# A GRU scan behind a mixture of experts: output turns placed behind the product of their window, one gate seed moved, and sixteen VectorE instructions in every step

## The chip, the cores and the metric

The kernel runs on one core of one Trainium2 chip. The metric is the device time of one execution in microseconds (us); the number that counts is the median over executions.

## The reference

The input `x` is [2, 1024, 256] in float32, with a condition vector of 256 per batch entry. Two layers follow, each added to its input:

```
# layer 0: four experts (two picked per batch entry) and a shared one
for e in range(E):                      # E = 4, hidden width 1024
    h = gelu(context_c @ ew1[e] + eb1[e])
    out = out + w_be[:, e] * mask[e] * (h @ ew2[e] + eb2[e])
out = out + gelu(context_c @ sw1 + sb1) @ sw2 + sb2
# layer 1: a GRU over the 1024 tokens, state h of 256 per batch entry
def step(h, xs):
    z = sigmoid(xzt + h @ U_z + vz)
    r = sigmoid(xrt + h @ U_r + vr)
    hh = tanh(xht + r * h @ U + vh)
    return (1.0 - z) * h + z * hh
```

The GRU is a chain of 1024 steps, and each needs the state that the step before it made.

## The kernel before

The 1024 tokens are cut into 16 chunks (`CH`) of 64 (`CT`). After a start of some 54 us, which computes layer 0 for chunk 0, the kernel runs one loop of 1024 steps. Step s is token t of chunk c. In each step TensorE multiplies the state by the three recurrent matrices (split into two float16 parts), and in two windows beside that it does the work of layer 0 for the next chunk: window 0 lies between the products of Z and those of C, window 1 lies behind the products of C. The list `SIDE[t, w]` says what stands in a window: one unit in window 0, two in window 1. Units are UP and DOWN (half a tile of the two expert matrices), BIAS, PROJECT (the input part of the gates) and IDLE.

The chain of one step runs over three engines. TensorE makes the sum of gate R; ScalarE takes its tanh (`gate_tanh`); VectorE makes `p_cur`, the reset state; TensorE multiplies it for gate C; ScalarE takes that tanh; VectorE's scan writes the new state `h_cur`. Gate Z goes beside it: `z_sum`, a tanh on ScalarE, and two instructions that write `blend`, from which the scan reads.

VectorE's own order in a step is: `p_cur` (L618), `z_sum` (L626), `p_low` (L629), a fill that clears a place in the bank of Z (L632), `blend` twice (L636 and L638), the scan (L644), `h_two` twice (L647 and L648, the second is the cast to float16), `half_h` (L649), and `out_feat` (L654). An instruction can carry one wait for a semaphore itself. Where the code asks for more, the others stand in wait instructions of VectorE's sequencer ahead of it, up to two semaphores in one. There are three of these in a step, at L617, L635 and L643, so a step has 14 instructions. The semaphore `blended` counts three times in a step: at each `blend` and at `half_h`. The semaphore `part_ready` counts six times: at `p_cur`, `p_low`, the fill, the scan, and the two `h_two`, the cast last (`H_HIGH16`).

Some steps have an instruction more on VectorE. `seed` copies a gate's bias over a bank of the next chunk, at the places named in `SEEDS`: (t, 1) is behind the blends of step t, (t, 0) is at the end of step t-1, behind `out_feat`. `residual` adds the sum of layer 0 to the features, twice per chunk. GpSimd multiplies the tiles of `hidden` by the expert weights (`scale_tile`, L283), after ScalarE's gelu.

Every 16 steps a TURN transposes the finished outputs on TensorE (`turn_body`, L758). It stands first in window 1 of t = 1, 17, 33 and 49, ahead of the window's one other unit, and it waits for `blended`, that is, for the second `blend` of its own step.

Of the kernel before, what the change touches and what calls it, by code (L numbers as in the profile page):

```python
# [15 lines left out]
P = 128  # L16
GATES = 3
R, Z, C = range(GATES)
# [14 lines left out]
H_FILL = 20  # L33
IDLE_FILL = (256, 384)
IDLE_AT = 128


def moe_gru_kernel(nc, x, cond, gate_w, gate_b, time_w, time_b, ew1, eb1, ew2, eb2, sw1, sb1, sw2, sb2,
                   w_z, u_z, c_z, b_z, w_r, u_r, c_r, b_r, w_h, u_h, c_h, b_h, branch_mask, out):
    B, T, D = x.shape  # L40
    E, _, H = ew1.shape
    BR = E + 1
    KC = D // P
    CT = TOKENS
    CH = T // CT
# [24 lines left out]


    FIRST_BRANCHES = [e for e in (0, 1, 3, 4, 2) if any(on for *_, on in token_ranges(0, e))]
    TILES = [[(e, j) for e in (FIRST_BRANCHES if c == 0 else range(BR)) for j in range(HT)] for c in range(CH)]
    TILE0 = [sum(map(len, TILES[:c])) for c in range(CH + 1)]
# [10 lines left out]
    UP, DOWN, BIAS, TURN, PROJECT, IDLE = "up", "down", "bias", "turn", "project", "idle"  # L85
    SIDE = {(t, w): [] for t in range(CT) for w in range(2)}
    TURNS = [(t, 1) for t in range(1, CT, STEPS)]
    for slot in TURNS:
        SIDE[slot].append((TURN, 0, 0))
    units = []  # L90
    for i in range(BR * HT + LAG):
        if i < BR * HT:
# [4 lines left out]
            units += [(DOWN, i - LAG, 0), (DOWN, i - LAG, 1)]  # L97
    for t in range(CT):
        for w in range(2):
            while units and len(SIDE[t, w]) < 1 + w:  # L100
                SIDE[t, w].append(units.pop(0))
                DOWN_STEP = t
    assert not units

    GELU_STEP = {}
# [4 lines left out]
    RESIDUAL_STEP = DOWN_STEP + 1  # L110
    projections = {w: [(g, m, k) for g in ((C,), (R, Z))[w] for m in range(KC) for k in range(KC)] for w in range(2)}
    for t in range(RESIDUAL_STEP + 1, CT):
        for w in range(2):
            while projections[w] and len(SIDE[t, w]) < 1 + w:
                SIDE[t, w].append((PROJECT, *projections[w].pop(0)))
    assert not any(projections.values())


    SEEDS = {(24, 0): (C, 0), (26, 0): (C, 1), (24, 1): (R, 0), (26, 1): (R, 1), (28, 1): (Z, 0), (30, 1): (Z, 1)}

    ROW_B1, ROW_BG, ROW_COND = 0, BR * HT, BR * HT + GATES * KC
    ROWS = ROW_COND + B * KC
# [2 lines left out]
    with ctx:  # L125
        def sb(name, shape, dt=F32):
            return ctx.enter_context(nc.sbuf_tensor(name, shape, dt))
# [4 lines left out]
        def sem(name):  # L132
            return ctx.enter_context(nc.semaphore(name))
# [29 lines left out]
        umax = sb("umax", [P, 1])  # L163
        table_probe = sb("table_probe", [P, 1])
        uall = sb("uall", [P, 1])
        w_scale = sb("w_scale", [P, 1])
        h_unscale = sb("h_unscale", [P, 1])
        half_s = sb("half_s", [P, ST])
# [54 lines left out]
        warm_made = sem("warm_made")  # L223
# [37 lines left out]
        z_summed = sem("z_summed")  # L261
        act_done = sem("act_done")
        part_ready = sem("part_ready")
        blended = sem("blended")
# [6 lines left out]
        PARTS_STEP = 6  # L271
        P_HIGH, P_LOW, Z_CLEAR, H_HIGH, H_LOW, H_HIGH16 = 1, 2, 3, 4, 5, 6

        BLEND_STEP = 3
# [161 lines left out]
        def _(dve):  # L436
# [125 lines left out]
            def seed(c, g, m):  # L562

                dve.tensor_copy(gate_v[g][:, c % 2, m, :, :],
                                gate_bias[:, g, m, :].unsqueeze(1).broadcast_to([P, CT, B])).then_inc(seeded, 1)
# [28 lines left out]
            def residual(c, k):  # L594
                if k == 0:
                    dve.wait_ge(down_done, TILE0[c + 1])
                here = feat[:, k, c * COLS:(c + 1) * COLS]
                dve.tensor_tensor(here, y_ps[:, k * COLS:(k + 1) * COLS], here, ALU.add).then_inc(feat_ready, 1)
# [4 lines left out]
            def side(c, t, window):  # L603
                if c == CH - 1:
                    return
                if (t, window) in SEEDS:
                    seed(c + 1, *SEEDS[t, window])
                if t == RESIDUAL_STEP:
                    residual(c + 1, window)

            sq = lambda ap: ap.rearrange("p (m b) -> p m b", b=B)
            for s in range(T):
                c, t = divmod(s, CT)
                parts = s * PARTS_STEP

                dve.wait_ge(act_done, s * GATES + R + 1)
                dve.wait_ge(part_ready, parts + H_HIGH)  # L617
                dve.scalar_tensor_tensor(p_cur[:, :, 0:B], sq(tanh_r), 1.0, sq(h_now), ALU.add, ALU.mult  # L618
                                         ).then_inc(part_ready, 1)

                dve.wait_ge(preact, s * GATES + Z + 1)
                here = gate_v[Z][:, c % 2, :, :, :]
                if t == 0:
                    dve.tensor_copy(sq(z_sum[:, :]), here[:, :, 0, :]).then_inc(z_summed, 1)
                else:
                    dve.tensor_reduce(sq(z_sum[:, :]), here[:, :, t - 1:t + 1, :].rearrange("p m t b -> p m b t"),  # L626
                                      AX.X, ALU.add).then_inc(z_summed, 1)
                dve.wait_ge(part_ready, parts + PARTS_STEP + P_HIGH)
                dve.tensor_tensor(p_low[:, :, 0:B], p_cur[:, :, 0:B], p_bits[:, :, 1:2 * B:2], ALU.subtract  # L629
                                  ).then_inc(part_ready, 1)  # L630
                dve.wait_ge(z_summed, s + 1)
                dve.memset(here[:, :, t, :], 0.0).then_inc(part_ready, 1)  # L632

                dve.wait_ge(act_done, s * GATES + Z + 1)
                dve.wait_ge(blended, (s + 1) * BLEND_STEP)  # L635
                dve.scalar_tensor_tensor(blend_v[:, :, 0], tanh_z, 1.0, half_s[:, :], ALU.add, ALU.mult  # L636
                                         ).then_inc(blended, 1)
                dve.scalar_tensor_tensor(blend_v[:, :, 1], tanh_z, 1.0, half_h[:, :], ALU.subtract, ALU.mult  # L638
                                         ).then_inc(blended, 1)
                side(c, t, 1)  # L640

                dve.wait_ge(act_done, s * GATES + C + 1)
                dve.wait_ge(blended, (s + 1) * BLEND_STEP + 2)  # L643
                dve.tensor_tensor_scan(h_cur[:, 0, :], cand, blend[:, :], 0.0, ALU.mult, ALU.add  # L644
                                       ).then_inc(part_ready, 1)
                dve.wait_ge(part_ready, parts + PARTS_STEP + H_HIGH)
                dve.tensor_tensor(h_low[:, 0, :], h_now, h_high, ALU.subtract).then_inc(part_ready, 1)  # L647
                dve.tensor_copy(h_high16, h_high).then_inc(part_ready, 1)  # L648
                dve.tensor_scalar(half_h[:, :], h_now, -0.5, None, ALU.mult).then_inc(blended, 1)  # L649

                body, row = divmod(s, STEPS)
                if row == 0 and body >= 2:
                    dve.wait_ge(turned, body - 1)
                last = dve.scalar_tensor_tensor(  # L654
                    out_feat[:, body % 2, :, row * B:(row + 1) * B], sq(h_now), h_unscale[:, :],
                    feat[:, :, s * B:(s + 1) * B], ALU.mult, ALU.add)
                if row == STEPS - 1:
                    last.then_inc(body_added, 1)

                if t < CT - 1:  # L660
                    side(c, t + 1, 0)

        @block.tensor
        def _(pe):
            mm = pe.matmul

            def idle(columns, bank=0, start=False):
                mm(up_ps[bank][:, IDLE_AT:IDLE_AT + columns], ident16[:, :], keep_warm[:, 0:columns],
                   start=start, stop=True, skip_group_check=True)
# [291 lines left out]
```

## Time and profile before

| what | value |
|---|---|
| median of 3 runs | 1899.76 us (1898.28 to 1903.29) |
| the profiled execution | 1901.32 us, span 1899.4 us |
| TensorE matmul, share of the span | 98% |
| TensorE weight load | 86% |
| VectorE | 77% |
| ScalarE | 38% |
| GpSimd | 10% |
| mean granted TensorE clock | 0.991 |

A busy TensorE isn't the same as a TensorE at its limit: matmuls overlap in its pipeline, and their ends are modelled. For a chain such as this one the useful views are the order in time of a few steps, and the spacing of one instruction that occurs once per step. In that order in time a row gives start, duration, engine, line, operation, and in brackets the idle time of the engine ahead of it with what ended it. The wait instructions of a sequencer are not counted as busy and are not in it.

### The profile page before, as it was taken

Reading aid. Unit: us, or ns where it says so; the run is one execution under the profiler, and the core shown is the slowest. Engines: PE = TensorE matmul, PEld = TensorE weight load, DVE = VectorE, ACT = ScalarE, POOL = GpSimd, SP = SyncE. Lnnn points to the kernel's source line nnn. Section 1 sums busy time; section 2 is a strip of 40 time slices with the busy share of each in tenths; the row PEclk is TensorE's granted clock in tenths of the full one; section 3 lists DMA queues with packets and bytes.
Section 4 is the critical chain, followed back from the end, with each engine's and each line's share of the span. In section 5 each row is a group of like instructions: output and inputs, shape, how many; then the busy total and the mean of one; then the engine's idle time right before and its main releaser. Section 6 shows DMA issues by size and latency. Waiting matters only on the chain.

```text
span 1899.4 us, 97811 instructions
## 1 busy us (share of the span) xinstructions
PE 1853.4 (98%) x38961; PEld 1633.5 (86%) x38962; DVE 1453.8 (77%) x11494; ACT 712.9 (38%) x3785; POOL 198.8 (10%) x515
## 2 busy tenths in 40 slices
PE   8999999999999999999999999999999999999988
PEld 8888888888898888988888888888988888888765
DVE  5687877778787786877778787787877878777776
ACT  4333433434333333333333334343433334333322
POOL 0110101101020110101101011010101101011000
PEclk9999999999999998999999999999999999999998
DMA  9000000000000000000000000000000000000000
GB/s 318 3 4 5 5 4 5 5 4 5 5 4 5 4 4 5 4 5 5 4 5 5 4 5 5 4 5 5 4 4 5 4 5 4 4 4 4 5 4 4
DMA packets 16903, 23.38 MB, mean 12 GB/s; under 512 B 3584, under 2 KB 15159, under 8 KB 16444
## 3 DMA queue, kind: packets, MB, share of 16 engines
q1 hardware_dynamic: 15280, 17.05, 2.6%
q8 instruction: 305, 5.00, 1.1%
q14 instruction: 154, 1.26, 0.2%
q10 hardware_dynamic: 1164, 0.07, 0.0%
HBM read 15.01 MB, written 2.10 MB: 9 GB/s over the span
## 4 chain that ended last, share of the span: by engine, by line
PE 89%; DVE 5%; ACT 3%; issue 2%; DMA 0%; SPq 0%; DVEq 0%
PE y_ps L736 18%; PE up_ps L718 18%; PE r_ps L841 13%; PE c_ps L841 12%; PE c_ps L820 6%; PE r_ps L820 6%; PE z_ps L841 5%; PE z_ps L850 4%; ACT rc_tanh_ps L403 3%; DVE h_cur L644 2%; DVE p_cur L618 1%; PE z_tanh_ps L758 1%; PE c_ps L752 1%; PE z_ps L752 1%; PE r_ps L752 1%
## 5 line engine op out<-in xcount | busy, mean ns | idle before, releaser
L718 PE MATMUL up_ps<-feat,up_w 128*128 128x128 f32 x2528 | 519.2, 302 | 0.3 <-DMA up_w<-in_L_cond_ew 0.3
L736 PE MATMUL y_ps<-hidden,down_w 128*128 128x128 f32 x2528 | 513.6, 300 | 0.0
L817 PEld LDWEIGHTS <-u_high 128*128 128x128 f16 x4096 | 400.7, 98 | 8.8 <-issue 0.8
L403 ACT ACTIVATE rc_tanh_ps<-r_ps 128x4 f32<-128x4 f32 x1024 | 161.8, 158 | 592.2 <-PE r_ps L841 592.1
L718 PEld LDWEIGHTS up_ps<-feat,up_w 128*128 128x128 f32 x2528 | 363.5, 190 | 1.4 <-ACT hidden L392 0.6
L736 PEld LDWEIGHTS y_ps<-hidden,down_w 128*128 128x128 f32 x2528 | 361.4, 190 | 0.4
L841 PEld LDWEIGHTS r_ps<-h_cur,u_mid 128*128 128x128 f16 x4096 | 253.5, 96 | 115.7 <-issue 54.4
L841 PEld LDWEIGHTS c_ps<-p_cur,u_mid 128*128 128x128 f16 x4096 | 253.5, 96 | 111.7 <-issue 33.3
L841 PE MATMUL r_ps<-h_cur,u_mid 128*128 128x20 bf16 (+5 forms) x4096 | 338.3, 179 | 0.0
L841 PE MATMUL c_ps<-p_cur,u_mid 128*128 128x40 bf16 (+10 forms) x4096 | 338.0, 180 | 0.0
L644 DVE TENSOR_TENSOR_SCAN h_cur<-rc_tanh_ps,blend 128x8 f32<-128x8 f32 x1024 | 177.7, 174 | 171.4 <-ACT rc_tanh_ps L403 169.8
L283 POOL TENSOR_TENSOR hidden<-hidden,expert_w 128x128 f32<-128x128 f32 (+3 forms) x416 | 163.5, 393 | 1357.6 <-ACT hidden L392 1357.6
L403 ACT ACTIVATE z_tanh_ps<-z_sum 128x4 f32<-128x4 f32 x1024 | 181.6, 177 | 311.2 <-DVE z_sum L626 305.7
L841 PE MATMUL c_ps<-p_cur,u_high 128*128 128x40 bf16 (+6 forms) x3072 | 287.3, 179 | 0.0
L841 PE MATMUL r_ps<-h_cur,u_high 128*128 128x20 bf16 (+3 forms) x3072 | 285.5, 178 | 0.0
L618 DVE SCALAR_TENSOR_TENSOR p_cur<-rc_tanh_ps,h_cur 128x4 f32<-128x4 f32 x1024 | 165.7, 162 | 151.7 <-ACT rc_tanh_ps L403 136.9
L649 DVE TENSOR_SCALAR half_h<-h_cur 128x4 f32<-128x4 f32 x1024 | 265.3, 259 | 0.0
L841 PE MATMUL z_ps<-h_cur,u_mid 128*128 128x20 bf16 (+5 forms) x4096 | 259.5, 178 | 0.0
L403 ACT ACTIVATE rc_tanh_ps<-c_ps 128x4 f32<-128x4 f32 x1024 | 161.8, 158 | 254.6 <-PE c_ps L841 254.6
L850 PE MATMUL z_ps<-h_two,u_high 128*128 128x20 f16 x4032 | 241.1, 169 | 0.2
L392 ACT ACTIVATE hidden<-up_ps,small_cols 128x128 f32<-128x128 f32 x632 | 231.1, 366 | 16.9 <-PE up_ps L718 15.6
L654 DVE SCALAR_TENSOR_TENSOR out_feat<-h_cur,h_unscale,feat 128x4 f32<-128x4 f32 x1024 | 222.7, 218 | 0.0
(151 smaller groups left out, 3765.2 us busy)
## 6 DMA issues: line engine op xcount, KB each, us to landing
up_w<-in_L_cond_ew SPq DMA_DIRECT2D x4, 1024.0 KB, 9.7
down_w<-in_L_cond_ew SPq DMA_DIRECT2D x4, 1024.0 KB, 10.3
x_rows<-in_x SPq DMA_DIRECT2D x8, 256.0 KB, 5.2
out<-out_rows SPq DMA_DIRECT2D x128, 16.0 KB, 1.8
up_w<-in_L_cond_sw SPq DMA_DIRECT2D x1, 1024.0 KB, 12.4
down_w<-in_L_cond_sw SPq DMA_DIRECT2D x1, 1024.0 KB, 13.2
cf<-in_L_cond_C_r SPq DMA_DIRECT2D x1, 256.0 KB, 9.7
cf<-in_L_cond_C_z SPq DMA_DIRECT2D x1, 256.0 KB, 9.9
```

The costliest lines, as they stand in the source:

```text
L392: act.activation(hidden[:, n % TILES_HELD, :], up_ps[n % 2][:, 0:COLS], ACT.Gelu_apprx_tanh, bias=small_cols[:, at:at + 1]).then_inc(gelu_ ...
L403: act.activation((tanh_r, tanh_z, c_now)[g].rearrange("p (m b) -> p m b", b=B), before_tanh, ACT.Tanh, scale=0.5 / GAIN).then_inc(act_done, 1)
L618: dve.scalar_tensor_tensor(p_cur[:, :, 0:B], sq(tanh_r), 1.0, sq(h_now), ALU.add, ALU.mult).then_inc(part_ready, 1)
L644: dve.tensor_tensor_scan(h_cur[:, 0, :], cand, blend[:, :], 0.0, ALU.mult, ALU.add).then_inc(part_ready, 1)
L649: dve.tensor_scalar(half_h[:, :], h_now, -0.5, None, ALU.mult).then_inc(blended, 1)
L654: last = dve.scalar_tensor_tensor(out_feat[:, body % 2, :, row * B:(row + 1) * B], sq(h_now), h_unscale[:, :], feat[:, :, s * B:(s + 1) * ...
L718: last = mm(up_ps[n % 2][:, 0:COLS], up_w[:, e, k, j * P:(j + 1) * P], feat[:, k, c * COLS:(c + 1) * COLS], start=(k == 0), stop=(k == KC ...
L736: last = mm(y_ps[:, m * COLS:(m + 1) * COLS], down_w[:, e, j, m * P:(m + 1) * P], hidden[:, n % TILES_HELD, :], start=False, stop=(m == KC ...
L817: pe.ldweights(w[:, g, k, m * P:(m + 1) * P])
L820: return pe.add_instruction(mybir.InstMatmult(name=nc.get_next_instruction_name(), engine=mybir.EngineType.PE, ins=[pe.lower_ap(moving), p ...
L841: return mm(gate_ps[g][:, at:at + width], w[:, g, k, m * P:(m + 1) * P], moving, start=False, stop=last_of_sum, skip_group_check=True)
L850: return mm(gate_ps[Z][:, at:at + width], w[:, Z, k, m * P:(m + 1) * P], h_two[:, 0:width // B, k * B:(k + 1) * B], start=False, stop=last ...
```

## The change

First, a TURN is put in its window behind the other unit instead of ahead of it; the number of units per window stays the same. Second, the two seeds of gate C at the end of a step go to the first even t from 22 on for which step t-1 has no gelu; these are 24 and 28 where it was 24 and 26. Third, VectorE's instructions in a step become 16. A one-column fill of `spare` stands ahead of `p_cur`, and it is left out where a seed or a residual has come in since the `p_cur` before. `p_cur` asks for four semaphores in place of two: the tanh of R as before, `part_ready` now up to the cast of the state, `blended` up to `half_h` of the step before (it stood at the first blend), and `z_summed` of the step before. The fill in the bank of Z asks for `p_low` as well. Ahead of the loop stand eight more one-column fills.

```
+LEAD_PADS = 8
-    for slot in TURNS:
-        SIDE[slot].append((TURN, 0, 0))
+    places = lambda t, w: 1 + w - ((t, w) in TURNS)
...
-            while units and len(SIDE[t, w]) < 1 + w:
+            while units and len(SIDE[t, w]) < places(t, w):
...
+    for slot in TURNS:
+        SIDE[slot].append((TURN, 0, 0))
-    SEEDS = {(24, 0): (C, 0), (26, 0): (C, 1), (24, 1): (R, 0), (26, 1): (R, 1), (28, 1): (Z, 0), (30, 1): (Z, 1)}
+    c_seeds = [t for t in range(22, CT, 2) if t - 1 not in GELU_STEP][:KC]
+    SEEDS = {**{(t, 0): (C, m) for m, t in enumerate(c_seeds)}, (24, 1): (R, 0), (26, 1): (R, 1), (28, 1): (Z, 0), (30, 1): (Z, 1)}
...
+            def extras(s):
+                c, t = divmod(s, CT)
+                between = ((t, 0), (t - 1, 1))
+                some = sum(slot in SEEDS or slot[0] == RESIDUAL_STEP for slot in between)
+                assert some <= 1
+                return some if c < CH - 1 else 0
+
+            for i in range(LEAD_PADS):
+                dve.memset(spare[:, 1 + i:2 + i], 0.0)
...
+                if extras(s) == 0:
+                    dve.memset(spare[:, 0:1], 0.0)
                 dve.wait_ge(act_done, s * GATES + R + 1)
-                dve.wait_ge(part_ready, parts + H_HIGH)
+                dve.wait_ge(part_ready, parts + H_HIGH16 if s else parts + H_HIGH)
+                dve.wait_ge(blended, (s + 1) * BLEND_STEP)
+                dve.wait_ge(z_summed if s else warm_made, max(s, 1))
                 dve.scalar_tensor_tensor(p_cur[:, :, 0:B], sq(tanh_r), 1.0, sq(h_now), ALU.add, ALU.mult
                                          ).then_inc(part_ready, 1)
...
                 dve.wait_ge(z_summed, s + 1)
+                dve.wait_ge(part_ready, parts + PARTS_STEP + P_LOW)
                 dve.memset(here[:, :, t, :], 0.0).then_inc(part_ready, 1)
 
                 dve.wait_ge(act_done, s * GATES + Z + 1)
-                dve.wait_ge(blended, (s + 1) * BLEND_STEP)
                 dve.scalar_tensor_tensor(blend_v[:, :, 0], tanh_z, 1.0, half_s[:, :], ALU.add, ALU.mult
```

## Rows read from the trace of the kernel before

**Rows 1.** The head of the page.

```profile
span 1899.4 us, 97811 instructions
```

**Rows 2.** One line's instructions, the scan: duration min/median/max, first and last start.

```profile
L644 DVE TENSOR_TENSOR_SCAN h_cur<-rc_tanh_ps,blend x1024: 162/174/175, 55.5 to 1894.9; 128x8 f32<-128x8 f32 x171
```

**Rows 3.** VectorE in order of time, a step without GpSimd.

```profile
705.97 0.17 DVE L644 TENSOR_TENSOR_SCAN h_cur<-rc_tanh_ps,blend 128x8 f32<-128x8 f32 x1 [0.17 <-ACT rc_tanh_ps L403]
...
706.33 0.16 DVE L649 TENSOR_SCALAR half_h<-h_cur 128x4 f32<-128x4 f32 x1
...
706.86 0.16 DVE L618 SCALAR_TENSOR_TENSOR p_cur<-rc_tanh_ps,h_cur 128x4 f32<-128x4 f32 x1 [0.25 <-ACT rc_tanh_ps L403]
...
707.06 0.17 DVE L629 TENSOR_TENSOR p_low<-p_cur 128x4 f16<-128x4 f32 x1
...
707.41 0.15 DVE L638 SCALAR_TENSOR_TENSOR blend<-z_tanh_ps,half_h 128x4 f32<-128x4 f32 x1
707.74 0.17 DVE L644 TENSOR_TENSOR_SCAN h_cur<-rc_tanh_ps,blend 128x8 f32<-128x8 f32 x1 [0.17 <-ACT rc_tanh_ps L403]
```

**Rows 4.** Two scans around a turn, and TensorE's turn and unit between them.

```profile
431.14 0.17 DVE L644 TENSOR_TENSOR_SCAN h_cur<-rc_tanh_ps,blend 128x8 f32<-128x8 f32 x1 [0.17 <-ACT rc_tanh_ps L403]
...
433.03 0.17 DVE L644 TENSOR_TENSOR_SCAN h_cur<-rc_tanh_ps,blend 128x8 f32<-128x8 f32 x1 [0.17 <-ACT rc_tanh_ps L403]
...
431.02 0.40 PE L758 MATMUL z_tanh_ps<-ident,out_feat 128*32 128x128 f32 x2
431.25 0.39 PE L718 MATMUL up_ps<-feat,up_w 128*128 128x128 f32 x2
```

**Rows 5.** VectorE in order of time, the step of the moved seed (t = 26).

```profile
100.42 0.17 DVE L644 TENSOR_TENSOR_SCAN h_cur<-rc_tanh_ps,blend 128x8 f32<-128x8 f32 x1 [0.18 <-ACT rc_tanh_ps L403]
...
101.41 0.14 DVE L618 SCALAR_TENSOR_TENSOR p_cur<-rc_tanh_ps,h_cur 128x4 f32<-128x4 f32 x1
```

**Rows 6.** The scan's stretch of low clock: busy (count), granted clock, DMA share, GB/s.

```profile
734.00:751.00 17.00, 1.39 (x8) 0.51 0.01 2
```

**Rows 7.** VectorE in order of time, step 14.

```profile
79.92 0.16 DVE L636 SCALAR_TENSOR_TENSOR blend<-z_tanh_ps,half_s 128x4 f32<-128x4 f32 x1
80.19 0.16 DVE L638 SCALAR_TENSOR_TENSOR blend<-z_tanh_ps,half_h 128x4 f32<-128x4 f32 x1
80.45 0.17 DVE L644 TENSOR_TENSOR_SCAN h_cur<-rc_tanh_ps,blend 128x8 f32<-128x8 f32 x1
```

**Rows 8.** VectorE in order of time, step 23.

```profile
96.26 0.15 DVE L638 SCALAR_TENSOR_TENSOR blend<-z_tanh_ps,half_h 128x4 f32<-128x4 f32 x1
96.86 0.17 DVE L644 TENSOR_TENSOR_SCAN h_cur<-rc_tanh_ps,blend 128x8 f32<-128x8 f32 x1 [0.46 <-ACT rc_tanh_ps L403]
```

**Rows 9.** DMA: instruction queue over the span; then 80.2 to 82 us in 40 slices.

```profile
q14 instruction: 154, 1.26, 0.2%
...
GB/s 0 0 0 0 0 0 0 0 0 0 0 0 0 0 182 0 0 0 0 0 0 0 0 0 0 0 0 0 0 0 0 0 0 0 0 0 0 0 0 0
```

**Rows 10.** Step 87: VectorE and GpSimd; DMA of 210.3 to 212.1 us in 40 slices.

```profile
210.10 0.17 DVE L644 TENSOR_TENSOR_SCAN h_cur<-rc_tanh_ps,blend 128x8 f32<-128x8 f32 x1 [0.18 <-ACT rc_tanh_ps L403]
...
210.46 0.38 DVE L649 TENSOR_SCALAR half_h<-h_cur 128x4 f32<-128x4 f32 x1
...
210.99 0.16 DVE L618 SCALAR_TENSOR_TENSOR p_cur<-rc_tanh_ps,h_cur 128x4 f32<-128x4 f32 x1
...
210.42 0.40 POOL L283 TENSOR_TENSOR hidden<-hidden,nothing 128x128 f32<-128x128 f32 x1 [1.38 <-ACT hidden L392]
...
GB/s 0 0 0 0 0 0 0 0 0 0 0 0 0 0 0 0 0 0 0 0 0 0 0 0 0 182 0 0 0 0 0 0 0 0 0 0 0 0 0 0
```

**Rows 11.** Wait instructions of VectorE's sequencer: one semaphore, and two.

```profile
L643 DVEq EVENT_SEMAPHORE  x1024: 21/21/21, 55.3 to 1894.7; - x171
...
L527 DVEq EVENT_SEMAPHORE  x1: 50/50/50, 24.0 to 24.0; - x1
```

**Rows 12.** The group of line L649: busy us, mean ns of one, idle before.

```profile
L649 DVE TENSOR_SCALAR half_h<-h_cur 128x4 f32<-128x4 f32 x1024 | 265.3, 259 | 0.0
```

More of the change, by code:

```diff
@@ L113, in moe_gru_kernel @@
         for w in range(2):
-            while projections[w] and len(SIDE[t, w]) < 1 + w:
+            while projections[w] and len(SIDE[t, w]) < places(t, w):
                 SIDE[t, w].append((PROJECT, *projections[w].pop(0)))
     assert not any(projections.values())
-    SEEDS = {(24, 0): (C, 0), (26, 0): (C, 1), (24, 1): (R, 0), (26, 1): (R, 1), (28, 1): (Z, 0), (30, 1): (Z, 1)}
+    for slot in TURNS:
+        SIDE[slot].append((TURN, 0, 0))
+    c_seeds = [t for t in range(22, CT, 2) if t - 1 not in GELU_STEP][:KC]
+    SEEDS = {**{(t, 0): (C, m) for m, t in enumerate(c_seeds)}, (24, 1): (R, 0), (26, 1): (R, 1), (28, 1): (Z, 0), (30, 1): (Z, 1)}
     ROW_B1, ROW_BG, ROW_COND = 0, BR * HT, BR * HT + GATES * KC
@@ L165, in moe_gru_kernel @@
         uall = sb("uall", [P, 1])
+        spare = sb("spare", [P, 1 + LEAD_PADS])
         w_scale = sb("w_scale", [P, 1])
```

## The prediction

> **What bounds the kernel now.** I read the page first, then the chain of waits, then a few steps in order of time, and last the spacing of the scan, which occurs once per step. The span is 1899.4 us [rows 1]. The scan starts first at 55.5 and last at 1894.9 [rows 2], so 1023 steps take 1839.4 us, 1.798 us each. An undisturbed step takes 1.77 us [rows 3]; over all scans in order of time the median is 1.777, and 1023 of those are 1817.9 us. This chain is serial, so the change can gain only from the 21.5 us by which steps exceed their median, or lose by making steps longer.
>
> I went through every scan's spacing to see which steps hold the 21.5 us:
>
> - Steps behind a turn: 5.8 us. In step t = 17 the turn starts at 431.02, its window's unit at 431.25, and scan to scan takes 1.89 us in place of 1.77 [rows 4]. There are 45 such steps at 0.11 us, 14 at t = 1 and 4 in the last chunk at 0.05.
> - The seed at t = 26: 1.2 us. `p_cur` starts 0.82 us after the scan's end [rows 5] where 0.72 is usual [rows 3]; 15 steps lose some 0.08.
> - Lower clock: 5.2 us in a few stretches. At a granted clock of 0.51, close to the 1.2 GHz level, 17 us hold 8 scans [rows 6]. The change has nothing to do with it.
> - VectorE's instructions coming late: 9.6 us. In step 14 the second blend starts 0.27 after the first [rows 7], usually 0.08. In step 23 the scan starts 0.45 us after the end of the blend that its wait instruction waits for [rows 8]; where only that wait held it, it was 0.10 [rows 7]. So something takes 0.35 us ahead of one instruction. Counting in program order, with 14 instructions a step, the blend of step 14 is number 203 of the loop and the scan of step 23 number 331 (from 0), 128 apart, and every other late one lies at one of the 113 places 75, 203, 331, ... The instruction queue moves 1.26 MB in 154 packets, 8 KB each, and one comes 0.67 us after the late blend's start [rows 9].
>
> **What a late instruction costs depends on where it falls.** Of the 113, 17 fall on the scan at 0.28 us each (4.8), 16 on the second blend at 0.12 (2.0), one on the first blend (0.2); steps behind these and behind a late cast lose 2.7, since the cast or `h_two` then meets GpSimd. The 13 on `p_cur` cost nothing: in step 87 `p_cur` starts on time, and the packet comes 0.44 us after its start [rows 10] in place of 0.67, so `p_cur` was ready some 0.23 us before it was due. The hold had its 0.35 us there: the wait instruction ahead of it (L617) asks only for the scan, whose end at 210.27 is 0.72 before `p_cur`. The sequencer doesn't run ahead over a wait instruction of its own; the late scan shows that, for its wait was released and only then did the 0.35 begin.
>
> **The change part by part.** *Turns.* The unit's two matmuls go into the time in which the turn waits for the blend (TensorE's last C product starts 0.27 us before the turn), and the turn starts as now and ends 0.22 earlier than the unit did. All but the last chunk's gain: 45 x 0.112 + 14 x 0.05 = **-5.7 us**. If the unit weren't done by then, the cost would be what it is now.
>
> *Seed.* Step 28 follows a step without gelu, `half_h` isn't held by GpSimd, and the copy ends before `p_cur` is due: **-1.2 us**.
>
> *Sixteen instructions.* The 113 places of now go: **-9.6 us**. With 16 a step, 128 are 8 steps, so each falls on one and the same place. Eight fills in front turn number 75 into 67 = 4 x 16 + 3: steps 4, 12, 20, ..., 128 of them, place 3. Place 0 is the fill, 1 and 2 are wait instructions (four waits: one carried, up to two in each of the others, as L527 has two [rows 11]), and place 3 is `p_cur`.
>
> That is the place that cost nothing, but the wait instructions ahead of it now ask for `half_h`. From `half_h`'s end to `p_cur` there are 0.37 us in a plain step (706.49 to 706.86) [rows 3] and 0.15 where GpSimd's product stretches `half_h` to 0.38 (210.84 to 210.99) [rows 10]. The trace has no pair of wait instructions in front of one instruction. From below it costs what one did, 0.10 [rows 7], and 0.02 more, the row of a wait itself; from above twice 0.10. I take 0.17: 0.10, plus 0.03 since two semaphores take 50 ns where one takes 21 [rows 11], plus 0.04 for the second.
>
> - Places where the sequencer is held: 0.17 + 0.35 = 0.52 us after `half_h`. Late by 0.15 in a plain step, by 0.37 in a stretched one. `half_h` has a mean of 259 ns [rows 12] between 164 and 388, so 0.42 of the steps are stretched. 74 x 0.15 + 54 x 0.37 = 11.1 + 20.0 = **+31.1 us** (24.7 to 34.9).
> - The other stretched steps, 0.42 x 896 = 380: 0.17 against 0.15 is 0.02 late: **+7.6 us** (0 to 19). The one-column fill in front, 0.06 long, lies in the same gap (`out_feat` ends just before `p_cur` there) and is bounded by the same 19.
> - The wait ahead of the bank's fill: 0.10 after `p_low`'s end at 707.23; the blends behind it then start up to 0.07 late. The second blend ends at 707.56, the scan comes at 707.74, 0.18 later, of which 0.10 is its own wait [rows 3, 7]. The 0.08 just covers it: **0**, and 1 us for each ns by which it doesn't.
> - The eight fills: once, ahead of the loop, while VectorE waits for the first sum: 0.
>
> Sum: -5.7 - 1.2 - 9.6 + 31.1 + 7.6 = **+22.2 us**. The profiled execution took 1901.32 us, 1.92 over its span and 1.6 above the median; on the median of 1899.76 the sum gives **1922 us**.
>
> **A page that would have it otherwise.** The rows show 8 KB per packet, 128 instructions apart, and 0.35 us that is seen wherever the sequencer has no lead. The Trainium skill (Runtime: NRT & Kernel Launch, Instruction fetch mechanics) has refills in blocks of 256 instructions and calls a crossing mostly hidden. By that the 16 would take away nothing and the places would cost nothing; it is the third rival.
>
> **The rivals.**
>
> 1. *Place 3 is as harmless as now.* If the sequencer decodes past the two waits before `half_h` is done, `p_cur` stands ready as in step 87. Then the 31.1 falls away, and the other stretched steps cost 0 to 0.01: 1899.8 - 16.5 + 0 to 8, **1887 us** with 1883 to 1893. For it: 13 places on `p_cur` without a loss, 14 on `p_low`. Against it: all 17 late scans began their 0.35 after their wait was released. It decides at whether the 0.35 starts before `half_h` ends by 0.15 or more.
> 2. *The places are harmless, the added waits aren't.* With 0.20 from `half_h` to `p_cur` and 0.05 lost in each of 434 stretched steps, 21.7 us come back: 1899.8 - 16.5 + 21.7 = **1905 us**, with 1896 to 1905 for less.
> 3. *Crossings are hidden in general* and the late instructions have another cause that the count doesn't move. Only turns and seed gain, and the waits cost 0 to 8: 1893 to 1901, say **1896 us**. Against it: no late instruction lies outside the 113 places.
> 4. *The idle time lowers the clock.* A stretch at half clock cost some 3.5 us (8 scans in place of 9.6 in 17 us [rows 6]). Added holes of 0.37 us on TensorE might bring five more of them: 1922 + 17 = **1939 us**. Against it: the 17 late scans left holes of 0.28 and the clock stayed.
>
> **How the numbers follow.** Forecast 0.64, own range 1908 to 1936. Rival 1: 0.22; rival 2: 0.06; rival 3: 0.04; rival 4: 0.04. About 0.3% (5.7 us) is what a measurement of this kernel can tell from no change. Faster is rival 1 and a little of 3: 0.23. Within is rival 2 and most of 3: 0.10. Slower: 0.67. The range 1888 to 1936 leaves out half of rival 1, rival 4 and the tails of the forecast.
>
> **What would show it.** In the changed kernel's order in time, every eighth step's `p_cur` should start 0.5 us after `half_h` ends and some 0.15 or 0.37 later than ScalarE's tanh allows; no scan and no blend should be late. Steps t = 18, 34, 50 should have the median spacing, t = 26 too. In stretched steps `p_cur` should come 0.05 after its tanh in place of 0.03. The forecast is wrong if `p_cur` of every eighth step is on time, if the late instruction falls on another place, or if the median step has become longer than 1.777 us, which would be the chain of the blends.

## The result, and the profile after

The changed kernel takes 1943.27 us (median of 4 runs, 1942.07 to 1944.02) where the kernel before takes 1899.02 (4 runs). The ratio is 1.0234 with a 95% interval of 1.0217 to 1.0251: slower by 44 us, twice the 22 of the forecast and 7 us above the upper end of its range. The lines of the changed file are used from here on: `p_cur` is L636, the bank fill L651, the blends L654 and L656, the scan L662, `half_h` L667, the spare fill L631, and the wait instructions stand at L634, L635, L650 and L661.

The page of the changed kernel: its head, the instruction queue, and three groups of VectorE (busy us, mean ns of one, then idle time ahead of it and what ended it).

```profile
span 1942.2 us, 99748 instructions
...
q14 instruction: 169, 1.38, 0.2%
...
L636 DVE SCALAR_TENSOR_TENSOR p_cur<-rc_tanh_ps,h_cur 128x4 f32<-128x4 f32 x1024 | 166.6, 163 | 194.3 <-ACT rc_tanh_ps L407 165.0
...
L662 DVE TENSOR_TENSOR_SCAN h_cur<-rc_tanh_ps,blend 128x8 f32<-128x8 f32 x1024 | 178.1, 174 | 147.6 <-ACT rc_tanh_ps L407 142.2
L667 DVE TENSOR_SCALAR half_h<-h_cur 128x4 f32<-128x4 f32 x1024 | 271.5, 265 | 0.0
```

The instruction queue has moved 15 packets more [rows 9], and `half_h` is nearly as long as it was [rows 12]. The idle time ahead of `p_cur` is 194 us. The steps themselves tell more. One line's instructions, the scan of the changed kernel: count, duration min/median/max, first and last start.

```profile
L662 DVE TENSOR_TENSOR_SCAN h_cur<-rc_tanh_ps,blend x1024: 173/174/175, 56.2 to 1937.7; 128x8 f32<-128x8 f32 x171
```

1023 steps take 1881.5 us in place of 1839.4 [rows 2], 1.839 each in place of 1.798. That is 42.1 of the 42.8 us by which the span grew [rows 1]: the loss lies in the steps, not ahead of the loop.

Now VectorE in order of time around `p_cur`, in three steps of the changed kernel: 596 (held, `half_h` short), 601 (not held, `half_h` stretched by GpSimd) and 612 (held and stretched).

```profile
1150.40 0.16 DVE L667 TENSOR_SCALAR half_h<-h_cur 128x4 f32<-128x4 f32 x1
...
1151.11 0.16 DVE L636 SCALAR_TENSOR_TENSOR p_cur<-rc_tanh_ps,h_cur 128x4 f32<-128x4 f32 x1 [0.42 <-ACT rc_tanh_ps L407]
...
1159.51 0.39 DVE L667 TENSOR_SCALAR half_h<-h_cur 128x4 f32<-128x4 f32 x1
...
1160.10 0.16 DVE L636 SCALAR_TENSOR_TENSOR p_cur<-rc_tanh_ps,h_cur 128x4 f32<-128x4 f32 x1
...
1179.67 0.39 DVE L667 TENSOR_SCALAR half_h<-h_cur 128x4 f32<-128x4 f32 x1
...
1180.61 0.16 DVE L636 SCALAR_TENSOR_TENSOR p_cur<-rc_tanh_ps,h_cur 128x4 f32<-128x4 f32 x1 [0.42 <-ACT rc_tanh_ps L407]
```

From the end of `half_h` to `p_cur` there are 0.55 us in both held steps (1150.56 to 1151.11, 1180.06 to 1180.61), and 0.20 in the one that is not held (1159.90 to 1160.10). In a plain step the usual distance is 0.37 [rows 3], in a stretched one 0.15 [rows 10]: so the held steps are late by 0.18 and 0.40 us, the stretched one by 0.05. The releaser named for the idle time is ScalarE's tanh, which in step 596 ended at 1150.90, 0.21 ahead of `p_cur`; the view names it because it shows no wait of the sequencer. That is the trap of this row: the tanh was over by then.

I took the distance from the tanh's end to `p_cur` in every one of the 1024 steps, and counted as late what is above the usual 0.033 us:

| steps | count | late each (mean) | sum | forecast |
|---|---|---|---|---|
| held (s = 4, 12, 20, ...), plain | 70 | 0.187 us | 13.1 us | 74 x 0.15 = 11.1 |
| held, `half_h` stretched | 58 | 0.406 us | 23.5 us | 54 x 0.37 = 20.0 |
| not held, stretched | 401 | 0.055 us | 22.1 us | 380 x 0.02 = 7.6 |
| not held, plain | 495 | 0.000 us | 0 us | 0 |

No scan and no blend is late any more. What the steps exceed 1.776 us by, once the late `p_cur` is taken off, is 6.0 us in place of 21.3. Of these 6.0, 2.9 lie in a place that the prediction doesn't name: the steps t = 61 and 62 of chunks 0 to 14 take 0.125 and 0.065 us longer. Most of the rest is low clock.

### The profile page after: what moved, and what is told of

Read it like the earlier page. It is cut to its first block, busy times and chain, and to the rows that moved or that the text cites. A ratio compares the mean times of both kernels' runs of the same rounds, so it can differ in the third digit from the quotient of the medians.

```text
span 1942.2 us, 99748 instructions
## 1 busy us (share of the span) xinstructions
PE 1882.3 (97%) x38962; PEld 1632.9 (84%) x38962; DVE 1397.2 (72%) x12406; ACT 713.6 (37%) x3785; POOL 199.4 (10%) x515
## 4 chain that ended last, share of the span: by engine, by line
PE 87%; DVE 6%; issue 4%; ACT 3%; DMA 0%; DVEq 0%; SPq 0%
PE y_ps L754 18%; PE up_ps L736 17%; PE c_ps L859 12%; PE r_ps L859 12%; PE c_ps L838 8%; PE r_ps L838 6%; PE z_ps L859 5%; PE z_ps L868 3%; ACT rc_tanh_ps L407 3%; DVE p_cur L636 2%; DVE h_cur L662 2%; PE z_ps L770 1%; PE r_ps L770 1%; PE up_ps L686 1%; DVE half_h L667 1%
## 5 line engine op out<-in xcount | busy, mean ns | idle before, releaser
L636 DVE SCALAR_TENSOR_TENSOR p_cur<-rc_tanh_ps,h_cur 128x4 f32<-128x4 f32 x1024 | 166.6, 163 | 194.3 <-ACT rc_tanh_ps L407 165.0
L662 DVE TENSOR_TENSOR_SCAN h_cur<-rc_tanh_ps,blend 128x8 f32<-128x8 f32 x1024 | 178.1, 174 | 147.6 <-ACT rc_tanh_ps L407 142.2
L667 DVE TENSOR_SCALAR half_h<-h_cur 128x4 f32<-128x4 f32 x1024 | 271.5, 265 | 0.0
L654 DVE SCALAR_TENSOR_TENSOR blend<-z_tanh_ps,half_s 128x4 f32<-128x4 f32 x1024 | 167.1, 163 | 137.1
## 6 DMA issues: line engine op xcount, KB each, us to landing
down_w<-in_L_cond_sw SPq DMA_DIRECT2D x1, 1024.0 KB, 13.1
```

## The experiments

**The place of the hold.** Eleven fills ahead of the loop move the hold from place 3, `p_cur`, to place 0, the spare fill. Nine move it to place 2, the wait instruction right ahead of `p_cur`.

```
-LEAD_PADS = 8
+LEAD_PADS = 11      # first experiment
+LEAD_PADS = 9       # second experiment
```

> The changed kernel with eleven fills ahead of the loop in place of eight, so that the hold of every eighth step falls on place 0, the spare fill, three places ahead of `p_cur`. Theory (the place costs): the hold of some 0.35 us is over before `half_h` ends, so the 128 held `p_cur` places lose their 36.6 us and only the wait chain of the stretched steps is left (some 459 steps x 0.055 = 25 us in place of 58.6): 1943 - 33 = 1910 us, and no `p_cur` over 0.25 us after the end of `half_h`. Rival (the added waits alone cost the time, and the place has no part in it): 1943 us, `p_cur` as late as in the changed kernel.

> The changed kernel with nine fills ahead of the loop, so that the hold falls on place 2, the two-semaphore wait ahead of `p_cur`. That wait can be fetched only once the wait at place 1, which waits for the end of `half_h`, has run. Theory (a hold behind a wait of its own cannot be covered): the held steps are as late as with place 3, `p_cur` some 0.5 us after `half_h`: 1943 us, between 1939 and 1947. Rival (only an instruction that computes is held, a wait can be passed): 128 holds vanish, 1910 us.

Measured: place 0 takes 1909.74 us (ratio to the kernel before 1.0046, 1.0031 to 1.0061), place 2 takes 1942.42 us (1.0215, 1.0200 to 1.0230). VectorE in order of time, steps 596 and 612, with the hold on place 0:

```profile
1131.27 0.16 DVE L667 TENSOR_SCALAR half_h<-h_cur 128x4 f32<-128x4 f32 x1
...
1131.81 0.16 DVE L636 SCALAR_TENSOR_TENSOR p_cur<-rc_tanh_ps,h_cur 128x4 f32<-128x4 f32 x1 [0.24 <-ACT rc_tanh_ps L407]
...
1160.17 0.39 DVE L667 TENSOR_SCALAR half_h<-h_cur 128x4 f32<-128x4 f32 x1
...
1160.76 0.16 DVE L636 SCALAR_TENSOR_TENSOR p_cur<-rc_tanh_ps,h_cur 128x4 f32<-128x4 f32 x1
```

`p_cur` comes 0.38 after `half_h` in step 596, as in a plain step, and 0.20 in step 612, as in any stretched step of this kernel. The same steps with the hold on place 2:

```profile
1150.31 0.16 DVE L667 TENSOR_SCALAR half_h<-h_cur 128x4 f32<-128x4 f32 x1
...
1151.03 0.16 DVE L636 SCALAR_TENSOR_TENSOR p_cur<-rc_tanh_ps,h_cur 128x4 f32<-128x4 f32 x1 [0.42 <-ACT rc_tanh_ps L407]
...
1179.60 0.39 DVE L667 TENSOR_SCALAR half_h<-h_cur 128x4 f32<-128x4 f32 x1
...
1180.56 0.16 DVE L636 SCALAR_TENSOR_TENSOR p_cur<-rc_tanh_ps,h_cur 128x4 f32<-128x4 f32 x1 [0.44 <-ACT rc_tanh_ps L407]
```

0.56 and 0.57 us. So three places of difference are worth 33.5 us (32.7 between places 2 and 0), and the waits alone are not the cause. The wait instructions themselves show where the hold lies. Those of step 596 in the changed kernel, then with the hold on place 2 (duration in ns, first and last start):

```profile
L634 DVEq EVENT_SEMAPHORE  x1: 21/21/21, 1150.6 to 1150.6; - x1
L635 DVEq EVENT_SEMAPHORE  x1: 49/49/49, 1150.7 to 1150.7; - x1
...
L634 DVEq EVENT_SEMAPHORE  x1: 21/21/21, 1150.5 to 1150.5; - x1
L635 DVEq EVENT_SEMAPHORE  x1: 50/50/50, 1150.9 to 1150.9; - x1
```

With place 3 the second wait starts 0.069 us after the first and `p_cur` 0.445 after the second; with place 2 it is 0.421 and 0.095 (medians of the held steps). Where nothing is held, in the stretched steps of the changed kernel, these are 0.069 and 0.095. So the same 0.35 us stands ahead of the very instruction that the count names, and behind the wait for `half_h` in both. A hold ahead of that wait is covered; a hold behind it, be it on a wait or on an instruction that computes, begins only when `half_h` has ended.

**The waits, with the place kept.** In the third experiment `p_cur` sits on place 3 of 16 as in the changed kernel, but its waits are on events that are over early, and the wait for `half_h` is back at the first blend. The wait for `p_low` ahead of the bank fill is gone.

```
-dve.wait_ge(part_ready, parts + H_HIGH16 if s else parts + H_HIGH)
-dve.wait_ge(blended, (s + 1) * BLEND_STEP)
+dve.wait_ge(part_ready, parts + H_HIGH)
 dve.wait_ge(z_summed if s else warm_made, max(s, 1))
+dve.wait_ge(warm_made, 1)
...
-dve.wait_ge(part_ready, parts + PARTS_STEP + P_LOW)      # ahead of the bank fill
...
+dve.wait_ge(blended, (s + 1) * BLEND_STEP)               # ahead of the first blend
```

> The changed kernel, still with 16 instructions in each step and the hold on place 3, but with the three waits ahead of `p_cur` on events that are over early (the scan's matrix copy, the previous `z_sum`, the warm-up), with the wait for `half_h` back at the first blend, and with no wait for `p_low` ahead of the bank fill. Theory (a wait that stays shut until `half_h` has ended is what makes place 3 and the stretched steps costly): `p_cur` is back at 0.03 us after its tanh or after `half_h`, the held steps too, the fill of the bank is back at 0.17 us behind `p_low`, and of the change only its gains are left: the sum of late places falls by 58.6 + 2.9 us: 1943 - 61 = 1882 us, from 1880 to 1888. Rival 1 (place 3 itself costs whatever is waited for): the 128 held steps keep 0.19 us and more each, 1882 + 24 = 1906 us or above. Rival 2 (the number of instructions per step is what costs): no change from 1943 us.

Measured: 1883.64 us (1883.12 to 1885.47), ratio 0.9908 (0.9892 to 0.9925), faster than both kernels. Steps 596 and 612 in order of time:

```profile
1115.04 0.16 DVE L667 TENSOR_SCALAR half_h<-h_cur 128x4 f32<-128x4 f32 x1
...
1115.58 0.16 DVE L636 SCALAR_TENSOR_TENSOR p_cur<-rc_tanh_ps,h_cur 128x4 f32<-128x4 f32 x1 [0.24 <-ACT rc_tanh_ps L407]
...
1143.46 0.39 DVE L667 TENSOR_SCALAR half_h<-h_cur 128x4 f32<-128x4 f32 x1
...
1144.00 0.16 DVE L636 SCALAR_TENSOR_TENSOR p_cur<-rc_tanh_ps,h_cur 128x4 f32<-128x4 f32 x1
```

0.38 and 0.15: on time in both, with the hold on the very same place. Over all steps no `p_cur` is late by more than 0.001 us. A hold that delays nothing can't be seen at `p_cur`, but the packet of the instruction queue shows it. DMA in 40 slices of 0.045 us around step 612, first the changed kernel from 1180.6 to 1182.4, then this one from 1144.0 to 1145.8:

```profile
GB/s 0 0 0 0 0 0 0 0 0 0 0 0 0 0 0 182 0 0 0 0 0 0 0 0 0 0 0 0 0 0 0 0 0 0 0 0 0 0 0 0
...
GB/s 0 0 0 0 0 0 0 0 0 0 0 182 0 0 0 0 0 0 0 0 0 0 0 0 0 0 0 0 0 0 0 0 0 0 0 0 0 0 0 0
```

Over the 128 held steps the packet comes 0.67 us after the start of `p_cur` in the changed kernel and 0.52 here (medians). If it follows the end of the hold by a fixed time, the hold is still there, and over some 0.15 us before `p_cur` is due. In this version neither place 3 itself nor the number of instructions costs anything; the wait that stays shut until `half_h` ends makes them cost.

**The same place rule on the scan.** The eighth experiment is this early version without the eight fills, so that the hold falls on place 11, the scan.

```
-LEAD_PADS = 8
+LEAD_PADS = 0
```

> The version with the early waits (1883.6 us, hold on place 3), without the eight fills ahead of the loop, so that in every eighth step the hold falls on place 11, the scan, right behind the wait for the second blend. Theory (a place is harmless when the wait ahead of it opens early, and costs what is left of the 0.35 us when that wait opens shortly before the instruction is due): each of the 128 held scans is late by 0.28 us as the 17 of the kernel before were: 1883.6 + 36 = 1919 us, between 1912 and 1924; no `p_cur` late. Rival (what the early waits gained has nothing to do with the place, so any place will do): 1884 us.

Measured: 1918.14 us (ratio 1.0087, 1.0066 to 1.0108). Second blend and scan of step 4 in order of time:

```profile
62.89 0.15 DVE L656 SCALAR_TENSOR_TENSOR blend<-z_tanh_ps,half_h 128x4 f32<-128x4 f32 x1
63.51 0.17 DVE L662 TENSOR_TENSOR_SCAN h_cur<-rc_tanh_ps,blend 128x8 f32<-128x8 f32 x1 [0.47 <-ACT rc_tanh_ps L407]
```

The scan starts 0.47 us after the end of the blend, as the late ones of the kernel before did with 0.45 [rows 8]. Of the steps 4, 12, 20, ..., 113 have a scan that is late, by 0.28 us each (32 us together), and no `p_cur` is late. The other 15 are t = 28 of chunks 0 to 14, and there the scan is on time: a seed behind the blends moves it to place 12, so that the hold falls on its wait instruction, behind no wait that opens late. The expectation counted all 128. The packet comes 0.67 us after the late scans, as it does after the late `p_cur` of the changed kernel. The place of the hold alone is worth 34 us between these two versions.

**GpSimd's part.** The fourth experiment takes the products of GpSimd out of chunks 1 to 15.

```
-pool.wait_ge(gelu_done, n + 1)
-scale_tile(pool, c, n, e, scaled)
+pass
...
-if e == E:
+if e == E or c > 0:                   # DOWN then waits for the gelu itself
     pe.wait_ge(gelu_done, n + 1)
```

> The changed kernel without GpSimd's multiplication of the expert tiles by their weights in chunks 1 to 15: this part of the computation is left out, so GpSimd has next to no work beside the scan. Theory (GpSimd's work stretches `half_h` from 0.16 to 0.39 us, and the wait chain then ends last): no step is stretched, the 401 x 0.055 us vanish and all 128 held steps cost 0.19 us: 1943 - 22 - 13 = 1908 us, `half_h` at 0.16 us throughout. Rival 1 (the stretch comes from elsewhere): `half_h` stays at 0.39 us in its steps and the time at 1943 us. Rival 2 (a held step costs the same whatever `half_h` does): 1943 - 22 = 1921 us.

Measured: 1915.5 us (ratio 1.0074, 1.0059 to 1.0089), 7.5 us above the expectation. `half_h` (L666 in this file) and the scan (L661), one line's instructions each:

```profile
L666 DVE TENSOR_SCALAR half_h<-h_cur x1024: 157/162/165, 61.7 to 1909.4; 128x4 f32<-128x4 f32 x171
...
L661 DVE TENSOR_TENSOR_SCAN h_cur<-rc_tanh_ps,blend x1024: 173/174/175, 61.3 to 1909.0; 128x8 f32<-128x8 f32 x171
```

The longest `half_h` is 165 ns, where the changed kernel has up to 395: the stretch is GpSimd's. 128 held steps are late by 0.183 us each (23.4 us), all others by nothing. In the steps, from the first scan to the last, the kernel loses 33.8 us against the changed one (1847.7 for 1881.5), and 35 were expected; 5.1 of the missing 7.5 us lie ahead of the loop, since the first scan comes at 61.3 in place of 56.2. The first select of GpSimd, which makes the matrix `ident`, and the first work of TensorE, which reads it, in the changed kernel and then here:

```profile
1.56 0.29 POOL L339 TENSOR_SCALAR_AFFINE_SELECT ident<-ident 128x128 f32<-128x128 f32 x1 [0.49 <-POOL ident L337]
4.46 1.08 PE L699 MATMUL rc_tanh_ps<-ident,x_rows 128*128 128x128 f32 x4 [4.46 <-DMA x_rows<-in_x]
...
8.84 0.28 POOL L339 TENSOR_SCALAR_AFFINE_SELECT ident<-ident 128x128 f32<-128x128 f32 x1 [7.78 <-issue]
9.53 1.12 PE L698 MATMUL rc_tanh_ps<-ident,x_rows 128*128 128x128 f32 x4 [9.53 <-POOL ident L342]
```

GpSimd starts its select 7.3 us later, and so TensorE starts 5.07 us later. What held GpSimd for these 7.78 us is not shown. The 5 us have no part in the steps. Rival 2 of this run (a held step costs the same whatever `half_h` does) would have left 13 us more in the steps.

**The order of the two waits.**

```
-dve.wait_ge(blended, (s + 1) * BLEND_STEP)
 dve.wait_ge(z_summed if s else warm_made, max(s, 1))
+dve.wait_ge(blended, (s + 1) * BLEND_STEP)
```

> The changed kernel with the two waits ahead of `p_cur` in the other order: the one on the previous `z_sum`, over early, now at place 1, and the one for `half_h` at place 2, so that after the end of `half_h` one own wait is left to run, not two. Theory (the two waits run one after the other behind `half_h`, 0.07 us apart): `p_cur` starts 0.13 us after `half_h` in place of 0.20, the stretched steps are no longer late (their 22 us vanish), the held steps are late by 0.12 and 0.34 us in place of 0.19 and 0.41 (36.6 becomes 28): 1943 - 31 = 1912 us. Rival (only their number matters, not their order): 1943 us.

Measured: 1915.93 us (ratio 1.0087, 1.0074 to 1.0101). Steps 601 and 612 of this version in order of time:

```profile
1143.30 0.39 DVE L667 TENSOR_SCALAR half_h<-h_cur 128x4 f32<-128x4 f32 x1
...
1143.83 0.16 DVE L636 SCALAR_TENSOR_TENSOR p_cur<-rc_tanh_ps,h_cur 128x4 f32<-128x4 f32 x1
...
1162.94 0.39 DVE L667 TENSOR_SCALAR half_h<-h_cur 128x4 f32<-128x4 f32 x1
...
1163.81 0.16 DVE L636 SCALAR_TENSOR_TENSOR p_cur<-rc_tanh_ps,h_cur 128x4 f32<-128x4 f32 x1 [0.35 <-ACT rc_tanh_ps L407]
```

The stretched step comes 0.14 after `half_h`, where the changed kernel has 0.20, and is on time; over all 401 of them the late sum is 0.1 us. The held one comes 0.48 after it. The late sum of all steps is 28.1 us, as expected (28); most of the 4 us between 1912 and the measured time lie in steps at low clock, which has seven short stretches within the loop of this execution (the mean granted clock is 0.989): they cost 6.9 us, where they cost 2.6 in the changed kernel. Two lines in another order are worth 27 us.

**The bank fill.** The seventh experiment keeps the wait ahead of the bank fill, but on an event that is over earlier.

```
-dve.wait_ge(part_ready, parts + PARTS_STEP + P_LOW)
+dve.wait_ge(part_ready, parts + PARTS_STEP + P_HIGH)
```

> The changed kernel with the wait ahead of the bank fill on `p_cur`'s copy, which is over 0.17 us earlier than `p_low`: still 16 instructions, all places the same. Theory (TensorE's first product of gate Z in the last two steps of a chunk waits for the fill, which the wait for `p_low` puts back by 0.14 us): steps t = 61 and 62 of chunks 0 to 14 lose their 0.125 and 0.065 us, 15 x 0.19 = 2.9 us: 1943.3 - 2.9 = 1940.4 us, and the fill starts some 0.17 us after `p_low` starts. Rival (these steps are late by what the turns or the seeds now do): 1943 us, t = 61 and 62 as in the changed kernel.

Measured: 1941.78 us (1939.91 to 1942.94; ratio 1.0223, 1.0209 to 1.0237). The medians alone, 1.5 us apart, don't settle 2.9 us. The traces do. Step 61 of the changed kernel in order of time, VectorE's bank fill and TensorE's work around it:

```profile
168.15 0.06 DVE L651 MEMSET z_ps<- 128x4 f32 x1
...
168.08 0.21 PE L859 MATMUL c_ps<-p_low,u_high 128*128 128x40 f16 x3
168.26 0.71 PE L770 MATMUL z_ps<-feat,wx 128*128 128x128 f32 x4
```

And of the seventh experiment:

```profile
168.08 0.06 DVE L651 MEMSET z_ps<- 128x4 f32 x1
...
168.15 0.21 PE L859 MATMUL c_ps<-p_low,u_high 128*128 128x40 f16 x3
168.23 0.69 PE L770 MATMUL z_ps<-feat,wx 128*128 128x128 f32 x4
```

In the changed kernel TensorE's projection of gate Z starts 0.18 us after the last products of C, 0.05 after the end of the fill; in the experiment 0.08 after them, the fill being over 0.09 before it. The code has the wait: a product of gate Z with k = 0 waits for `part_ready` up to `Z_CLEAR`, which the fill counts. The fill starts 0.309 us after `p_low` in the changed kernel and 0.171 here, and t = 61 and 62 are at the usual spacing in all 15 chunks. This is the cause of these 2.9 us.

**Turns and seed alone.** The kernel before with its 13 or 14 instructions and its own waits, and only these two of the change:

```
+places = lambda t, w: 1 + w - ((t, w) in TURNS)
...
+for slot in TURNS:                       # after the units and the projections
+    SIDE[slot].append((TURN, 0, 0))
+c_seeds = [t for t in range(22, CT, 2) if t - 1 not in GELU_STEP][:KC]
```

> The kernel before with the order of the turns and the moved seed of the changed kernel alone: no fills, no added waits, 13 or 14 instructions per step as before. Theory: the two moves are worth what the trace of before shows for them, 45 x 0.112 + 14 x 0.05 + 1.2 = 6.9 us: 1899 - 7 = 1892 us, the steps behind a turn at the median, the other late places of the kernel before still there. Rival (the turn's cost moves to the product that now stands ahead of it, or the seed's to t = 22): 1899 us.

Measured: 1891.73 us against 1898.50 (ratio 0.9961, 0.9949 to 0.9974), 4.9 to 9.7 us faster. Two scans and the turn of the step that is shown in [rows 4]; the scan is L656 and the turn L770 in this file:

```profile
430.11 0.17 DVE L656 TENSOR_TENSOR_SCAN h_cur<-rc_tanh_ps,blend 128x8 f32<-128x8 f32 x1 [0.17 <-ACT rc_tanh_ps L407]
431.89 0.17 DVE L656 TENSOR_TENSOR_SCAN h_cur<-rc_tanh_ps,blend 128x8 f32<-128x8 f32 x1 [0.17 <-ACT rc_tanh_ps L407]
...
430.05 0.38 PE L770 MATMUL z_tanh_ps<-ident,out_feat 128*32 128x128 f32 x2
```

1.78 us in place of 1.89, with the turn 0.06 ahead of the scan where it was 0.12. t = 26 is at the usual spacing too.

## Why the prediction was right in its mechanism and wrong in its size

**What bounds the kernel** held. 42.1 of the 42.8 us lie in the chain of the steps. Other engines have a part only through that chain: GpSimd by the stretch of `half_h`, TensorE by the bank fill.

**Turns and seed, -6.9.** Right: the run with these two alone shows 4.9 to 9.7 us, and the steps named are at the usual spacing.

**The 113 places, -9.6.** Right as far as it can be told: the early version has the turns, the seed and the 16 instructions, and stands at 0.9908 of the kernel before where turns and seed alone stand at 0.9961; 0.53% of 1899 is 10 us, with intervals of some 3 us on either side.

**The held places, +31.1.** The place, the count and the 0.35 us were right, and so was the sentence that decided against rival 1, that the sequencer doesn't run ahead over its own wait. The size was 36.6. Two things add up: 0.202 us from `half_h` to `p_cur` where I took 0.17, and 58 stretched steps among the held for 54.

**The other stretched steps, +7.6.** This is the step that failed: 22.1 were lost, above the 19 of its own upper bound. The whole term hangs on the difference between the chain of waits and the 0.15 us that it has to fit into, and I chose 0.17 between bounds of 0.12 and 0.20. The trace has 0.202 (0.038 from the end of `half_h` to the first wait instruction, 0.069 to the second, 0.095 to `p_cur`). So each is late by 0.055 and not by 0.02, nearly three times as much, from an error of 0.03 us, and there are 401 of them for 380. The order of the waits shows where I erred: I priced the second wait at 0.04 on top of the first, as if they overlapped for the most part, but the two run one after the other, and one of them less gives back 0.06 to 0.07. The other parts of the price were right: the swapped version has one wait of two semaphores behind `half_h`, and its held steps show 0.484 us, that is 0.13 beside the 0.35, where I had 0.10 + 0.03. The very price was in the text, in rival 2 (0.20 and 0.05 in 434 steps), as a case for a chance of 0.06 and without the held places. Forecast and rival 2 were not exclusive: the kernel shows the holds of the one with the wait price of the other.

**The bank fill, 0.** Right for the blends: the first of them starts 0.02 us later after its tanh, and the scan still starts at its usual 0.033 us after the tanh of C. Wrong as a whole, because I followed the fill only to the instructions behind it on VectorE and not to the other reader of its semaphore: TensorE's projection of gate Z lost 2.9 us.

**The sum.** -6.8 (the medians with turns and seed alone) - 9.6 + 36.6 + 22.1 + 2.9 = 45.2, against 42.8 in the spans; the low-clock stretches account for most of the difference, 5.2 us before and 2.6 after. Of the 23 us between this sum and the forecast's 22.2, 14.5 are the stretched steps, 5.5 the held places and 2.9 the bank fill. At the upper ends of my own bounds the terms would have given -16.5 + 34.9 + 19 = +37, or 1937 us: my range stopped at 1936, short of what its own bounds allowed.

**The rivals.** Rival 1 falls with the hold on places 2 and 3 against place 0: the sequencer doesn't pass the wait for `half_h`. Its 1887 us is near the early version's 1883.6, but by another way, since there no wait ahead of `p_cur` asks for `half_h`. Rival 2's price was right and its claim on the places wrong. Rival 3, crossings hidden in general, falls with the eight fills that move 34 us between the two early versions. The rule of the Trainium skill that stood beside it (Runtime: NRT & Kernel Launch, Instruction fetch mechanics: a crossing is mostly hidden) agrees with these traces only where the wait ahead of the held place opens early. Rival 4 didn't occur: the granted clock is 0.991 before and after.

**The signs named ahead.** Every eighth `p_cur` at 0.5 us after `half_h`, no late scan, t = 18, 34, 50 and 26 without their old excess: all seen. In stretched steps `p_cur` was to come 0.05 us after its tanh, and it comes 0.09 after: that is the step that failed. A median step above 1.777 us was to mean that the chain of the blends had grown, and that sign misled: the median is 1.831, but it is that of a stretched step, since 520 of the steps are late (all 128 held ones and 392 of the 401 others that are stretched).

## What to carry to other kernels

In these traces a wait instruction of its own is a wall for VectorE's instruction stream: what stands behind it, the periodic hold of 0.35 us too, starts only when it opens. (That the hold is the loading of instructions is inferred from the packets that follow it; no run changes the loading itself.) So let the wait instructions ahead of an instruction on the chain ask for what is over early; put the wait that opens last behind the other waits, or at a later instruction with slack; and place a periodic hold ahead of the wall. When a price has to be taken between two bounds and hundreds of steps sit right at the edge of their slack, a difference of 0.03 us decides: then let the range hold what the upper bound costs over all these steps. And follow every reader of a semaphore that is moved, on all engines.

## What was not expected of the hardware

Two wait instructions in a row cost one after the other even when the second is already met (the cast, the later of the two events that it asks for, ends 0.07 us before `half_h`): 0.069 us from the first (one semaphore) to the second (two semaphores), 0.095 from that to the instruction. One line's instructions, the two waits of the changed kernel: duration min/median/max in ns, first and last start.

```profile
L634 DVEq EVENT_SEMAPHORE  x1024: 21/21/21, 51.4 to 1936.3; - x171
...
L635 DVEq EVENT_SEMAPHORE  x1024: 49/50/50, 51.5 to 1936.4; - x171
```

The durations shown, 21 and 50 ns, are well under half of what the pair costs from `half_h`'s end to `p_cur` (0.202): the rest lies around them and is in no view. And the hold proved exact: with 16 instructions in a step it falls on the same place in all 128 of its steps, and the number of one-column fills ahead of the loop, 0.06 us each, sets what it costs. With the waits of the changed kernel the held steps lose 36.6 us with 8 fills, and with 11 the 3 that the pair of waits costs in them; in the early version they lose nothing with 8 and 32 us with none.
